# A macaron block on one core: the division of attention moved from PE transposes to a round trip through DRAM, the output product three periods later

## What is computed

```python
x = x + 0.5 * _L0_ffn_ref(_layernorm(x), w1, b1, w2, b2)   # ternary weights, gelu, 256 -> 1024 -> 256
x = x + _L0_attn_ref(_layernorm(x), Wq, Wk, Wv, Wo)
x = x + 0.5 * _L0_ffn_ref(_layernorm(x), w1, b1, w2, b2)
```

## Time and profile before

| | |
|---|---|
| median of three runs | 602.37 us |
| span of the profiled execution | 600.8 us |
| its own time | not given apart from the span |
| PE busy | 567.2 us (94%) |
| DVE, ACT, POOL busy | 458.9 (76%), 345.2 (57%), 229.3 us (38%) |
| DMA | 63.45 MB, mean 106 GB/s |
| first feed-forward, attention, second feed-forward | about 0 to 151, 151 to 477, 477 to 601 us |

### The profile page before, as it was taken

One profiled execution on the slowest core, in us unless ns is written; L12 is line 12 of the kernel. 1 busy time (PEld: TensorE's weight loads), 2 busy tenths in 40 slices (PEclk: granted clock), 3 DMA queues, 4 the chain that ended last, 5 costly groups with the idle time before them and its releaser, 6 DMA issues.

```text
span 600.8 us, 17866 instructions
## 1 busy us (share of the span) xinstructions
PE 567.2 (94%) x6596; PEld 496.4 (83%) x6596; DVE 458.9 (76%) x928; ACT 345.2 (57%) x610; POOL 229.3 (38%) x446
## 2 busy tenths in 40 slices
PE   1999999999789999999999999999888999999998
PEld 1789999999668888888888888888665788999997
DVE  5977777779797978879788788877562777777765
ACT  2765454546246666776667766567545655455453
POOL 6383333332665354444544445434141033333310
PEclk9999999999999999999999999999989999999999
DMA  6530000000987567654576546765400011111111
GB/s 221 199 112 6 0 0 0 0 0 1 257 219 207 167 164 208 172 157 146 166 204 177 158 139 175 197 186 159 138 2 3 1 36 35 35 35 35 35 35 36
DMA packets 71190, 63.45 MB, mean 106 GB/s; under 512 B 4178, under 2 KB 64370, under 8 KB 71154
## 3 DMA queue, kind: packets, MB, share of 16 engines
q1 hardware_dynamic: 69970, 62.81, 36.1%
q10 hardware_dynamic: 1184, 0.14, 0.2%
HBM read 33.03 MB, written 29.36 MB: 104 GB/s over the span
## 4 chain that ended last, share of the span: by engine, by line
PE 82%; DVE 10%; DMA 3%; ACT 2%; issue 1%; POOL 1%; SPq 1%; ACTq 0%; DVEq 0%
PE bank L173 18%; PE bank L537 18%; PE bank L1065 13%; PE bank L673 6%; PE bank L1060 6%; PE bank L1121 5%; PE bank L1196 4%; PE bank L1161 3%; PE bank L156 2%; PE bank L1124 2%; PE bank L1134 2%; DVE mx L863 2%; DVE g_lo L257 2%; PE bank L1184 1%; DMA w1f<-w1t 1%
## 5 line engine op out<-in xcount | busy, mean ns | idle before, releaser
L863 DVE TENSOR_REDUCE mx<-bank 128x2 f32<-128x512 f32 (+1 forms) x192 | 118.7, 684 | 31.3 <-PE bank L1065 31.2
L240 ACT ACTIVATE g<-bank,b1c 128x512 f32<-128x512 f32 x128 | 88.0, 690 | 65.6 <-PE bank L173 62.5
L537 PE MATMUL bank<-w2q,g_hi 128*128 128x256 f32 x512 | 124.4, 284 | 1.3 <-DVE g_lo L257 0.9
L537 PE MATMUL bank<-w2q,g_lo 128*128 128x256 f32 x512 | 122.5, 280 | 0.0
L985 ACT ACTIVATE probs<-bank 128x512 f32<-128x512 f32 x192 | 111.2, 597 | 11.9 <-PE bank L1065 4.4
L537 PEld LDWEIGHTS bank<-w2q,g_hi 128*128 128x128 f32 x512 | 96.5, 188 | 2.9 <-DVE w2q L375 1.1
L537 PEld LDWEIGHTS bank<-w2q,g_lo 128*128 128x128 f32 x512 | 96.5, 188 | 0.6
L315 POOL TENSOR_TENSOR res<-res,b2h 128x1024 f32 (+1 forms) x16 | 38.3, 2394 | 133.0 <-DVE xn L147 128.9
L257 DVE TENSOR_TENSOR g_lo<-g,g_hi 128x512 fp32r<-128x512 f32 x128 | 82.8, 689 | 3.1
L173 PE MATMUL bank<-xt_hi,w1q 128*128 128x512 f32 x240 | 77.3, 404 | 2.0 <-DVE xt_lo L167 2.0
L173 PE MATMUL bank<-xt_lo,w1q 128*128 128x512 f32 x240 | 76.4, 400 | 0.0
(11 more groups left out here) (129 smaller groups left out, 1170.1 us busy)
## 6 DMA issues: line engine op xcount, KB each, us to landing
qk_slots<-parts SPq DMA_DIRECT2D x32, 384.0 KB, 3.6
q<-qk_slots SPq DMA_DIRECT2D x32, 384.0 KB, 4.0
k<-qk_slots SPq DMA_DIRECT2D x32, 384.0 KB, 4.5
qk_slots<-parts SPq DMA_DIRECT2D x32, 256.0 KB, 3.4
res<-x SPq DMA_DIRECT2D x8, 512.0 KB, 3.6
qk_slots<-parts SPq DMA_DIRECT2D x32, 128.0 KB, 3.2
out<-res SPq DMA_DIRECT2D x7, 512.0 KB, 2.9
w1f<-w1t SPq DMA_DIRECT2D x2, 512.0 KB, 6.1
```

Of the source, the lines that this page charges most:

```text
L240: nc.scalar.activation(g[:, f, :], of[:], ACT.Gelu, bias=b1c[:, f:f + 1]).then_inc(g_ready, 1)
L537: last = nc.tensor.matmul(to[:, 0:D], part[:, f, t * P:(t + 1) * P], w2q[:, f, :], start=f == 0 and part is g_hi, stop=f == FC - 1 and par ...
L863: nc.vector.tensor_reduce(o, i, AX.X, ALU.max).then_inc(s_done, 1)
```

## The change

The transposes around the division go. Every one of the 16 pad columns is now one. ACT copies the bank of `PV` to `o_sb`, SP stores it to DRAM (`store_heads`, two DMAs a period), loads the rows of the sums alone as 128 x 32 (`load_den`, two), DVE inverts them (`reciprocals`), SP stores these (`store_rden`) and in the next period loads the heads in the layout that the product with Wo wants (`load_output`) and the inverted sums, each repeated over 16 rows. DVE multiplies the two (`normed_heads`), ACT and DVE split as before, from SBUF. The rows of Wo are put in the order of the heads on the host. The product with Wo of sequence b stands in period b+3 instead of b+1; those of the last three sequences stand in the first three chunks of the second feed-forward, into `o_bank`. Periods -2 to 3 are now written out, and the loop has three rounds (4 to 9). The masks are 128x128 with a repeated axis in the access pattern, the small constant rows lie in `by_cos`, and buffers move so that all fits. In ACT's last period the gelus 2 and 3 stand ahead of `copy_heads`.

```diff
+        rden_dram = nc.dram_tensor("rden_slots", (BATCH, 2, 4 * KC * SEQ), F32, kind="Internal").ap()
+        heads_dram = nc.dram_tensor("head_slots", (BATCH, 2, 4, 2 * HD, KC * SEQ), F32, kind="Internal").ap()
...
-        mask_qk = sb("mask_qk", [P, 4, P], BF16)
-        mask_kq = sb("mask_kq", [P, 4, P], BF16)
+        mask_qk = sb("mask_qk", [P, P], BF16)
+        mask_kq = sb("mask_kq", [P, P], BF16)
         ones_mean = sb("ones_mean", [P, P])
-        minus_rows = sb("minus_rows", [PARTS, SEQ], BF16)
-        fence_q, fence_k = sb("fence_q", [FENCE, SEQ], BF16), sb("fence_k", [FENCE, SEQ], BF16)
+        att_t = [sb(f"att_t{n}", [P, KC, SEQ], F32R) for n in ("_hi", "_lo")]
...
+        few = by_cos[0:PARTS, 0, :].bitcast(BF16)
+        fence_q, fence_k, minus_rows = (few[:, i * SEQ:(i + 1) * SEQ] for i in range(3))
+        rows_in = [sem(f"att_rows_in{p}") for p in range(2)]
+        parts = [sb("parts0", [P, 2, PARTS, 2 * SEQ], BF16)]
+        den, rden = (sb(n, [P, 2, KC * SEQ * 4 // P]) for n in ("den", "rden"))
+        o_sb, att, rden_rows = (sb(n, [P, KC * SEQ]) for n in ("o_sb", "att", "rden_rows"))
...
                     def turn_first():
+                        for rows in rows_in:
+                            dve.wait_ge(rows, 48)
...
+                        late = phase == 1 and isinstance(c, int) and c < 3
...
+                            if late and c == 0 and f == FC - 3:
+                                of_last.reciprocals(dve)
+                        if late:
+                            of_last.normed_heads(dve, c)
                         low_part(dve, gc, FC - 1, first)
...
                         dve.wait_ge(xb_ready, gc + 1)
+                        if late:
+                            of_last.low_att(dve, c)
                         for t in range(CT):
...
                                     if phase == 0 and not before:
                                         dve.wait_ge(x_in, 16 * c + 48)
                                     ln_stats(ahead)
+                                if late:
+                                    of_last.add_output(dve, c)
...
-                        with dve.Fori(1, LAST - 1) as c:
+                        chunk(1, 2, 3)
+                        chunk(2, 3, 4)
+                        with dve.Fori(3, LAST - 1) as c:
...
+                            if phase == 1 and isinstance(c, int) and c < 3:
+                                of_last.copy_att(act, c)
...
+                            if phase == 1 and not opening and f == 3:
+                                pe.wait_ge(wo_done, BATCH - 2 + c if isinstance(c, int) and c < 3 else BATCH + 1)
...
+                        if phase == 1 and isinstance(c, int) and c < 3:
+                            of_last.output(pe, c)
...
-FIRST, LOOPED, AFTER = -2, (1, 5), 17
+FIRST, LOOPED, AFTER = -2, (4, 3), 17
...
+        def reciprocals(dve, p):
+            dve.wait_ge(den_in, 32 * p.p)
+            if p.has(-2):
+                dve.wait_ge(rden_out, 16 * (p.p - 1))
+            nc.vector.reciprocal(rden[:], den[:]).then_inc(den_s, 1)
+
+        def normed_heads(dve, p):
+            dve.wait_ge(heads_in, 16 * (p.p - 2))
+            dve.wait_ge(rden_in, 16 * (p.p - 2))
+            nc.vector.tensor_tensor(att[:], att[:], rden_rows[:], ALU.mult).then_inc(normed, 1)
+
+        def copy_att(act, p):
+            act.wait_ge(normed, p.p - 2)
+            nc.scalar.copy(att_t[0][:].rearrange("p k s -> p (k s)"), att[:]).then_inc(att_hi_s, 1)
+
+        def low_att(dve, p):
+            dve.wait_ge(att_hi_s, p.p - 2)
+            nc.vector.tensor_tensor(att_t[1][:].rearrange("p k s -> p (k s)"), att[:],
+                                    att_t[0][:].rearrange("p k s -> p (k s)").bitcast(F32), ALU.subtract).then_inc(att_lo_s, 1)
+
+        def output(pe, p, to=mixed[1]):
+            pe.wait_ge(att_lo_s, p.p - 2)
+            if to is o_bank:
+                pe.wait_ge(o_copied, 2 * BATCH)
+            elif p.has(3):
+                pe.wait_ge(v_done, p.p + 4)
+            else:
+                pe.wait_ge(wo_done, p.p - 2)
+            for t in range(QT):
+                for n, (w, a, k) in enumerate(PASSES):
+                    last = nc.tensor.matmul(to[:, t * D:(t + 1) * D], att_t[a][:, k, t * P:(t + 1) * P], wo[w][:, k, :],
+                                            start=n == 0, stop=n == len(PASSES) - 1)
+            last.then_inc(wo_ready, 1)
+
+        def add_output(dve, p, of=mixed[1]):
+            b = p.p - 3
+            dve.wait_ge(wo_ready, b + 1)
+            nc.vector.tensor_tensor(res[:, bass.ts(b, QT), :], of[:].rearrange("p (t d) -> p t d", t=QT),
+                                    res[:, bass.ts(b, QT), :], ALU.add).then_inc(wo_done, 1)
...
+            def store_heads(p, h):
+                sp.wait_ge(o_copied, 2 * p.p + h)
+                sp.dma_start(heads_dram[p.p - 1 + h, 1 - h].rearrange("j r s -> (j r) s"), o_sb[:]).then_inc(o_stored, 16)
+
+            def load_den(p):
+                sp.wait_ge(o_stored, 32 * p.p)
+                for half in range(2):
+                    sp.dma_start(den[:, half, :], heads_dram[p.p - 1, half, :, HD, :]).then_inc(den_in, 16)
+
+            def store_rden(p):
+                sp.wait_ge(den_s, p.p - 1)
+                sp.dma_start(rden_dram[p.p - 2].rearrange("h (p c) -> p h c", p=P), rden[:]).then_inc(rden_out, 16)
+
+            def load_output(p):
+                b = p.p - 2
+                if p.known and p.has(-3, 0, BATCH):
+                    sp.wait_ge(att_lo_s, p.p - 2)
+                sp.dma_start(att[:], heads_dram[b, :, :, 0:HD, :]).then_inc(heads_in, 16)
+                sp.wait_ge(rden_out, 16 * (p.p - 1))
+                sp.dma_start(rden_rows[:], rden_dram[b].rearrange("h (j s) -> h j s", j=4).unsqueeze(2)
+                             .broadcast_to([2, 4, HD, KC * SEQ])).then_inc(rden_in, 16)
...
+                if p.has(-1) if h == 0 else p.has(0):
+                    store_heads(p, h)
+                if h == 0 and p.has(-2):
+                    store_rden(p)
                 if p.has(2):
                     load(p, h)
+                if h == 0 and p.has(-1):
+                    load_den(p)
+                if h == 1 and p.has(-2):
+                    load_output(p)
...
+            store_rden(Period(BATCH + 1))
+            load_output(Period(BATCH + 1))
...
-                if p.has(1):
-                    maxima(p, h)
+                last = p.known and p.p == BATCH
                 if h == 0:
+                    if p.has(1):
+                        maxima(p, 0)
                     if opening:
                         statistics(p.turn(5))
                         rope(p)
+                    if p.has(-3) and not last:
+                        normed_heads(dve, p)
                     if p.has(4, 2):
                         normalise(p)
+                    if p.has(-3) and not last:
+                        low_att(dve, p)
                     if p.known and p.p == BATCH - 2:
                         dve.wait_ge(wo_done, 3)
                         ln_stats(0)
-                    if p.known and p.p == BATCH:
+                    if last:
                         then.low_part(dve, CHUNKS, 0)
                         then.cast_by_dve(dve, CHUNKS, 1)
                         then.low_part(dve, CHUNKS, 1)
-                    if p.has(-1):
-                        normed_heads(p, 0)
                     if p.known and p.p == BATCH - 1:
                         ln_stats(1)
                     if p.has(3) and not opening:
...
                     if p.known and p.p == BATCH - 2:
                         ln_apply(dve, 0, following)
                 else:
+                    if p.has(1):
+                        maxima(p, 1)
+                    if p.has(-1) and not last:
+                        reciprocals(dve, p)
                     if p.par == 1 and p.has(5, 2, BATCH - 2) and not opening:
                         statistics(p.turn(5))
-                    if p.has(-1):
-                        low_att(p)
-                    if p.known and p.p == BATCH:
+                    if last:
                         then.cast_by_dve(dve, CHUNKS, 3)
                         then.low_part(dve, CHUNKS, 2)
                         then.low_part(dve, CHUNKS, 3)
                     if p.has(3):
                         take_rest(p, 0)
                         take_rest(p, 1)
-                    if p.has(0):
-                        normed_heads(p, 1)
                     if p.has(4, 2):
                         low_xt(p)
-                    if p.has(-1):
-                        add_output(p)
+                    if p.has(-3) and not last:
+                        add_output(dve, p)
...
-                j = 2 * p.p + h - 1
-                act.wait_ge(pv_done, j + 1)
-                nc.scalar.copy(o_sb[:].rearrange("p g s -> p (g s)"), o_bank[:]).then_inc(o_copied, 1)
+                act.wait_ge(pv_done, 2 * p.p + h)
```

(45 more changed lines are left out.)

134 lines of the change are left out of this document (43 added, 91 removed).

## The result

The changed kernel takes 598.59 us in the median of six runs (596.78 to 600.72), the kernel before 602.36 (602.0 to 603.21). The ratio is 0.9935, with a 95% interval from 0.9916 to 0.9955: faster by 3.8 us, where 11.1 was forecast. The profiled execution took 599.17 us, its span is 597.4. Two things stand out before any detail is read. The six runs spread over 3.9 us where those before spread over 1.2, and TensorE's mean granted clock in them is 0.982 to 0.991 of full speed. The profiled execution before has 0.997, and the later runs of that kernel have 0.991 to 1.00.

What follows compares the result with a forecast made beforehand. PE, busy 18.65 of 18.76 us a period, was taken as the bound. Terms 8.6 + 0.4 + 3.0 + 1.5 + 1.0 + 1.4 + 3.8 - 4.3 - 3.3 - 1.0 = 11.1 us gave 591.3 us, range 584 to 601.

Steps and rivals of the forecast that it cites:

- The ten periods, 8.6: Attention periods 3 to 12: each saves 0.41 in half 0 and 0.45 in half 1, 8.6 us in all.
- Periods 1 and 2 with period 0, 3.4: Start of attention: period 0 loses one transpose group, 0.4; periods 1 and 2 also lose WO, 1.5 each, 3.0.
- Period 13, 1.5, and period 14, 1.0: End of attention: period 13's WO, without V, starts earlier, 1.5; period 14 loses transposes but its statistics come later, 1.0.
- The second feed-forward, -4.3, -3.3 and -1.0: Costs there: three output products -4.3, last reciprocals delaying the first chunk -3.3, later normalisation in chunks 1 and 2 -1.0.
- the stall of 3.3: First chunk of the second feed-forward: late last reciprocals hold low parts, transposes at 20.0 where 16.7 was possible, -3.3 us.
- Ends of period 15, 1.4 and 3.8: Period 15: half 0's wait behind transposes goes, 1.4; half 1 to the second products takes 12.4 for 16.3, 3.8.
- The clock: Granted clock of TensorE: noted as 1.00 in the period of attention read; the sum has no term for it.
- rivals 2 and 3: Heads' round trip: 2, a new wait eats most, near 599, chance 0.12; 3, it sets the period, slower, 609, 0.13.
- Rival 2: Steady periods: DMAs land in 4.0 us each, loop 18.4, ten periods save 0.3 each; near 599; chance 0.12.
- the loop through DRAM: Heads stored, sums loaded, on to the next stores: 16.1 us on average, under 17.9, so priced at nothing.
- none of the four: Rivals: 1 nearly all kept, 584.5 (0.18); 2 near 599 (0.12); 3 slower, 609 (0.13); 4 hardly matters, 600 to 603 (0.07).
- No ACT wait on stored heads: Sign of being right: ACT copies the next heads without waiting; stored heads land at 7.8, wanted at 8.5.

Runs made afterwards that it cites:

- the statistics first: Changed kernel with DVE taking chunk 0's statistics in period 14 ahead of the heads product and low part: 595.74 us.
- with them in period 13: Changed kernel with chunk 0's statistics and moments in half 1 of period 13, its normalisation ahead of period 14's heads product: 592.3 us, ratio 0.9831.
- the second profile: The changed kernel measured again with no edit: 599.32 us, ratio 0.992 to the kernel before.
- Three short edits: Changed kernel; last reciprocals in FFN2 chunk 1, chunk 0's statistics and normalisation in period 13, heads product behind POOL's split in periods 13 and 14: 586.26 us.
- the kernel made to idle: Kernel before with 24 small POOL fills ahead of the first split of the maxima in periods 11 and 12: 610.14 us, ratio 1.0117.

## Why the prediction was wrong

**Sum and mechanism.** The time lies inside the range and on the forecast side, but the forecast of 591.3 missed by 7.3 us. Three steps failed. The sum has no term for the clock (3.3 us by the slope). Periods 13 and 14 were priced without the queue behind the new wait on DVE (2.5 forecast, -0.9 measured). Period 3 was taken for a steady one (0.9 forecast, -2.6 measured). The last two figures contain the falls of the clock that lie in these periods. In the terms of the sum:

- *The ten periods, 8.6.* Right for nine of them (7.5 for 7.7): half 0 keeps its 0.41 and half 1 gives back what the wait for V's copy takes, 0.33. Period 3 alone lost 2.6. The term counted period 3 as one of the steady ones. A gap of 1.7 to 2.5 us stands in it, whose cause stays open (moving the loop's border alone did not bring it about in the kernel before), and even without it period 3 takes 19.1 us or more in every variant, against 17.9 for the later ones: the waits for the rows of the maxima and for ACT shown above.
- *Periods 1 and 2 with period 0, 3.4.* 4.9, towards the upper bound.
- *Period 13, 1.5, and period 14, 1.0.* These failed: 0.6 and -1.5. The step read "the head product and the low part, 1.9 later" and then "I get 17 us for 18". The delay was right (the statistics start 1.99 us behind the product's start) but the product itself waits 0.7 to 1.9 us for its rows, and the period had been 19.60 and not 18. The maxima of half 1 queue behind the normalisation, and PE waited 2.2 to 5.2 us in the five profiles that keep this order and have no dummies. The experiments price it: 1.3 us at full clock for the statistics first, 4.4 with them in period 13, of which a part is period 3's. Also missed was that a product with both operands in SBUF holds up POOL (0.85 us). DVE's heads product had been priced by its own duration, 0.69, which was right (0.68), and not by what it does to a neighbour.
- *The second feed-forward, -4.3, -3.3 and -1.0.* Right: 8.4 for 8.6, and 3.1 for the stall of 3.3 when it was taken away.
- *Ends of period 15, 1.4 and 3.8.* Right, 1.4 and 4.1.
- *The clock.* This is the largest miss, and the prediction has no term for it. It noted a granted clock of 1.00 for the steady periods and carried it to the whole. All the terms count what PE has to do at 2.4 GHz. In its profiled run the changed kernel idles for 1.7 to 2.5 us in six places from the first scores to the first chunk of the second feed-forward, and behind four of them 3.4 or 6.8 us go at 1.2 GHz (five falls in the second profile): by the slope 3.3 us of the gain in the mean over 12 runs. The trace before had the sign of it, one fall in period 14 behind waits of 1.09 and 0.54 us.

In the profiled execution 7.7 us are missing: 2.6 at the start, 3.5 in period 3, 3.4 in periods 13 and 14 and 0.2 in periods 4 to 12, less 2.0 gained elsewhere. It spent 17.1 us at 1.2 GHz, the one before 3.4; by the slope that is 4.4 of them, and waits are the other 3.3. The start's 2.6 is a fall of 6.8 us and 0.2 of k's rows landing later; in the other profiles with the same code there that wait was 1.3 to 2.5 us, and in those of the kernel before without dummies 1.8 to 2.1, with a fall of 3.4 us behind it in one of three. So the wait is scatter and no cost of the change. Whether the fall is one is not settled: seven of the eight profiles of the changed kernel and its variants without dummies have one that begins between 161 and 171.

**Rivals.** The mechanisms of rivals 2 and 3 did not come about: periods 4 to 12 take 17.9 us each. What the prediction held against the change from the Trainium skill ("DMA: Bandwidth & Descriptors", Specifications: transfers below 512 bytes are read, modified and written) did not set the period either. The trace agrees that such rows are slow for their size: the inverted sums, 16 KB in rows of 64 bytes, landed after 3.0 us in the median of nine, in the DMA table from 248 to 400 us, where the 256 KB of the heads took 2.7. Whether the rewriting or the queue is the reason is not shown.

```profile
rden_slots<-rden SPq DMA_DIRECT2D x9, 16.0 KB, 3.0
```

Rival 2 had the time, near 599, but by other ways than it named: the landings and the loop through DRAM cost the steady periods nothing. Taken by its mechanism none of the four came about.

**What was to be seen.** PE is busy 98% in periods of 17.83 us, the waits for V's copy are 0.33, DVE waited 2.44 us for the last sums, three output products stand in the second feed-forward: as said. "No ACT wait on stored heads" was wrong:

```profile
ACT o_sb L1052 <- DMA head_slots<-o_sb: 8.7, 6, 1.7
```

Six waits, up to 1.7 us, with the store landing after 2.8 us in the median as against 3.2 in the sum. (What the prediction has from the Trainium skill, "DMA: Bandwidth & Descriptors", Anatomy of one DMA, 2.0 us plus the bytes at 436 GB/s and so an estimate of 2.6, is stated there for DMAs issued by GpSimd; SP issues these.) What was off is the issue: in period 7 the store of maxima goes out at 306.76 and the heads' at 307.80, 5.25 us after the period's start, where the sum had 4.6. In the loop these waits hide on ACT, and only beside the one in period 13 did PE wait, 0.27 us.

## What to carry over

Price a stall of a busy TensorE at its length plus its clock: on this kernel each fall went with 1.1 us more. Three short edits were worth 11.6 us in the mean (12.8 in the median). Of these PE's waits in the last periods and the first chunk after them are 5.2 (12.3 us in the profile of the changed kernel, 7.1 in that of the three edits), the clock 4.3 by the slope, and period 3's gap, absent there, some 2. When something is moved behind a new wait on one engine, follow everything that is queued behind it (here statistics, normalisation, maxima) and what the neighbour engine does in that moment, above all in the periods where the pipeline runs empty. Compare versions at equal granted clock before a difference of a few microseconds is explained, and look at the spread: the changed kernel's runs scatter with a standard deviation of 2.0 us (12 runs), those of the kernel before with 1.2 (56 runs).

## What the hardware showed that was not expected

- TensorE's clock fell behind short pauses. Waits of 1.4 to 2.5 us on an engine that was busy before and behind were followed by a stretch of 3.4 us at 1.2 GHz (2.46 and 2.27 us in the kernel made to idle, a fall behind both in its profile). Others of the same length passed without: 2.54 us in period 13 brought a fall in one profile of the changed kernel and none in another. Falls came in lengths of 3.4 and 6.8 us.
- Four to seven dummy products of 512 columns in such a wait hold the clock: the mean goes from 0.995 to 0.999 in the kernel before and from 0.987 to 0.994 in the changed one, at no measurable cost (0.1 us at full clock in the first, 0.9 within the errors in the second).
- POOL's instructions of 0.22 us took 0.59 and 0.70 beside a DVE product and a DVE subtraction that read both operands from SBUF; over the whole kernel the last step of the split went from a mean of 228 to 453 ns. In the steady periods PE is busy for 98% all the same.
- TensorE paused for 1.7 to 2.5 us with no releaser, beside instruction packets, in some layouts of nearly the same code and not in others.
